# A three-way split output product, a full-height warm-up and a new order of jobs in a fused attention and quaternion kernel

## The reference, cut to what matters

```python
qkv = x @ Wqkv.T + bqkv
attn = softmax(q @ k.T / 4)
coh = sigmoid(tanh(concat(x, cond) @ Wc1.T + bc1) @ Wc2.T + bc2)
mod = attn * coh / (sum(attn * coh) + 1e-8)
fa = softmax(layernorm(relu(cond @ We1.T) @ We2.T) @ pe.T)
mod = (1 - 0.21) * mod + 0.21 * fa
x1 = x + (mod @ v) @ Wout.T + bout
out = x1 + rotate(gate(x1))
```

## Time and profile before

| what | us |
|---|---|
| median of 3 runs | 286.6 |
| lowest and highest | 285.88, 288.35 |
| the profiled execution, device time | 284.87 |
| its span, first to last instruction | 282.2 |
| mean granted clock of TensorE | 0.994 |

### The profile page before, as it was taken

One profiled execution on the slowest core, in us unless ns is written; L12 is line 12 of the kernel. 1 busy time (PEld: TensorE's weight loads), 2 busy tenths in 40 slices (PEclk: granted clock), 3 DMA queues, 4 the chain that ended last, 5 costly groups with the idle time before them and its releaser, 6 DMA issues.

```text
span 282.2 us, 4292 instructions
## 1 busy us (share of the span) xinstructions
PE 258.2 (92%) x1579; PEld 127.6 (45%) x1579; DVE 197.8 (70%) x232; ACT 168.7 (60%) x214; POOL 158.0 (56%) x143
## 2 busy tenths in 40 slices
PE   8999898989989878998989989989998999899984
PEld 7446543433544333635444444445453444344333
DVE  5689878557758567577677858876788677758323
ACT  3341654757566854475755884567656677586850
POOL 3950499999999499998000099980024079910000
PEclk9999999999979999999999999999999999999999
DMA  7854543300191005631270003400302500101002
GB/s 208 277 175 146 181 135 114 114 2 3 53 251 35 1 0 146 178 90 38 77 244 21 1 9 111 144 2 2 112 1 99 165 0 31 48 1 38 2 0 74
DMA packets 16787, 23.49 MB, mean 83 GB/s; under 512 B 2488, under 2 KB 8504, under 8 KB 16768
## 3 DMA queue, kind: packets, MB, share of 16 engines
q1 hardware_dynamic: 15936, 22.55, 26.1%
q10 hardware_dynamic: 832, 0.69, 0.8%
HBM read 8.41 MB, written 2.11 MB: 37 GB/s over the span
## 4 chain that ended last, share of the span: by engine, by line
PE 68%; ACT 11%; DVE 10%; issue 6%; DMA 2%; POOL 1%; ACTq 1%; SPq 0%; DVEq 0%; POOLq 0%
PE o_ps L1109 16%; PE job_ps L862 15%; PE pair_ps L1082 11%; ACT probs L541 9%; PE pair_ps L1094 8%; DVE maxima L686 5%; PE job_ps L996 4%; PE pair_ps L862 2%; DMA w_raw<-wqkvT 2%; PE job_ps L932 2%; DVE qk_lo L702 2%; PE pair_ps L970 1%; PE job_ps L962 1%; ACTq L585 1%; ACT max_rows L581 1%
## 5 line engine op out<-in xcount | busy, mean ns | idle before, releaser
L686 DVE TENSOR_REDUCE maxima<-pair_ps 128x2 f32<-128x1024 f32 x128 | 153.0, 1220 | 52.4 <-PE pair_ps L1082 51.9
L541 ACT ACTIVATE probs<-pair_ps 128x1024 f32<-128x1024 f32 x128 | 125.8, 1024 | 44.1 <-PE pair_ps L1094 37.0
L1109 PE MATMUL o_ps<-probs,vals 128*32 128x512 f32 x512 | 68.2, 604 | 0.2
L1094 PE MATMUL pair_ps<-stack 49*128 49x512 f32 x256 | 53.9, 441 | 6.0 <-ACT probs L541 3.9
L1082 PE MATMUL pair_ps<-stack 48*128 48x512 f32 x256 | 54.5, 446 | 2.6 <-ACT probs L541 1.5
L1094 PEld LDWEIGHTS pair_ps<-stack 49*128 49x128 f32 x256 | 24.0, 185 | 27.4 <-ACT probs L541 10.4
L1082 PEld LDWEIGHTS pair_ps<-stack 48*128 48x128 f32 x256 | 24.0, 186 | 24.0 <-issue 12.5
L400 POOL TENSOR_TENSOR x_lo<-x_raw,x_hi 128x1024 fp32r<-128x1024 f32 x3 | 7.1, 2373 | 46.2 <-ACT x_hi L547 46.2
L417 POOL TENSOR_TENSOR vals<-v_new,row 128x256 f32<-128x256 f32 x16 | 11.4, 732 | 32.8 <-ACT v_new L573 20.1
L516 POOL TENSOR_TENSOR prod<-amap,x_tok 128x1024 f32<-128x1024 f32 x12 | 28.5, 2377 | 0.9
L1109 PEld LDWEIGHTS o_ps<-probs,vals 128*32 128x32 f32 x512 | 10.1, 108 | 20.9 <-issue 19.6
(11 more groups left out here) (159 smaller groups left out, 305.3 us busy)
## 6 DMA issues: line engine op xcount, KB each, us to landing
stack<-qk_hi SPq DMA_DIRECT2D x64, 128.0 KB, 2.9
stack<-qk_lo SPq DMA_DIRECT2D x32, 128.0 KB, 2.9
x_tok<-x SPq DMA_DIRECT2D x4, 512.0 KB, 4.3
out<-y SPq DMA_DIRECT2D x8, 256.0 KB, 2.4
x_raw<-xT SPq DMA_DIRECT2D x3, 512.0 KB, 5.4
fa_now<-fa_rows SPq DMA_DIRECT2D x4, 256.0 KB, 3.5
row<-rows SPq DMA_DIRECT2D x1, 544.0 KB, 5.6
x_raw<-xT ACTq DMA_DIRECT2D x1, 512.0 KB, 4.9
```

Source lines behind the costliest of these rows:

```text
L541: nc.scalar.activation(probs[:, t % 4, :, :], ps[:, :, :], ACT.Exp, scale=SCALE).then_inc(exp_done, 1)
L686: nc.vector.tensor_reduce(maxima[:, gg % 2, :, pair, i], pair_ps[SLOT["S", u]][:, :, :], AX_X, ALU.max, negate=True).then_inc(s_reduced, 1)
L1094: ins = nc.tensor.matmul(pair_ps[SLOT["T", t]][:, a, :], stack[64 * a:64 * a + ROWS + 1, 1, p, j * P:(j + 1) * P], stack[64 * a:64 * a + R ...
L1109: ins = nc.tensor.matmul(o_ps[h * VW:(h + 1) * VW, :], vals[:, j, gg % G * HG + h, :], probs[:, (2 * k + h // 2) % 4, h % 2, :], start=(j ...
```

## The change

- The output product of batches 0 to 2 is a `split_product`: GpSimd splits `oT` (two halves of features for each batch) and `wf` into high and low parts, and TensorE runs three single passes. The parts of `oT` lie in the two columns of `stack` that the direct products used. The splits stand in GpSimd's order after the step of the next batch that OUT_SPLIT_STEPS names. The last batch keeps the fp32 product.
- `y` lies in `w_raw` instead of in a tensor of its own.
- The warm-up's ones have 128 rows, and TensorE starts when they are written.
- The q and k weights are split by ScalarE (high) and VectorE (low) instead of by GpSimd; a memset of `stack` moves from VectorE to GpSimd.
- All lists of runs, jobs and weighings are replaced; LATE is empty; X_HIGH_PAUSE is 3 instead of 6, HEAD 12 instead of 13, FORE_PAUSE 40 instead of 43.

In the new lists (first pauses again 0, 26, 48, 70), `out0` and `out1` stand in pauses 46 and 56 for batch 0 (39 and 44 before), 74 and 77 for batch 1 (61 and 68), and 96 and 99 for batch 2 (83 and 90).

```diff
@@ -36,34 +36,37 @@
-FIRST_RUNS = ("- S SS SS SS SS S SS TSTST SS TS S TSSSS T TS S ST TT TT TS ST TTS ST S STT TS").split()
-RUNS = ("TSS STT TSS SST STS TST TST TST SST TSTTS SS TST ST TSS STT TST STS STS STT ST STT ST").split()
-LAST_RUNS = ("STS TST STS STT STS TSS TSTS TST TSS STT ST TST TTS STS ST TSSTS STT ST T TST TSS TSS").split()
-TAIL_RUNS = ("TT T T T T T T TT TT").split()
...
-JOB_PAUSES = {"q0": -15, "k0": -13, "v0": -10, "q1": -5, "k1": -2, "v1": 0, "coh0": 2, "coh1": 3, "max0": 5,
-              "z": 7, "max1": 10, "zt": 14, "tok0": 15, "max2": 16, "field": 16, "max3": 22, "tok1": 23,
-              "back0": 26, "tok2": 28, "tok3": 31, "back1": 34, "out0": 35, "out1": 42}
-FIRST_PAUSES = {"dq0": 0, "dk0": 0, "q0": 0, "k0": 1, "dq1": 2, "dk1": 2, "cond": 2, "v0": 3, "q1": 4, "k1": 5,
-                "max0": 6, "coh0": 6, "v1": 7, "norms": 7, "fpre": 8, "coh1": 9, "max1": 12, "fpair": 12,
-                "z": 17, "max2": 18, "zt": 19, "tok0": 19, "flog": 20, "tok1": 23, "max3": 27, "field": 30,
-                "tok2": 32, "back0": 32, "tok3": 34, "back1": 37, "out0": 39, "out1": 44}
-LAST_PAUSES = {"q0": -14, "k0": -12, "v0": -5, "q1": -4, "v1": 2, "k1": 3, "max0": 5, "coh0": 7, "coh1": 8,
-               "max1": 11, "max2": 15, "field": 15, "z": 16, "zt": 18, "tok0": 19, "max3": 22, "tok1": 24,
-               "back0": 27, "tok2": 31, "tok3": 42, "back1": 48, "out0": 85, "out1": 86}
...
-WEIGH_AFTER = [1, 2, 1, 1, 0, 1, 1, 0, 1, 1, 2, 2, 0, 1, 0, 0]
-LAST_WEIGH_AFTER = [1, 0, 0, 2, 1, 1, 2, 1, 2, 0, 2, 3, 1, 0, 0, 3]
-HEAD = 13
+FIRST_RUNS = ("- SS SS SS SS SSS STSS STTST STSTS SST TSS ST ST TTS ST ST T T S S T S T T S T").split()
+RUNS = ("STS STS STS STS TST STS TSTSTS STT TTS TST TST TSTSS TTS TST TST STS SSS ST TT S TS T").split()
+LAST_RUNS = ("STS TSS STS TST STS STS TSTS STS TST TST TST STS TS TST TST STS ST TTS STS T S T TS S T T").split()
+TAIL_RUNS = ("TT TT TT T T T T T T").split()
...
+JOB_PAUSES = {"q0": -16, "k0": -14, "q1": -11, "coh0": -7, "v0": -6, "k1": 0, "coh1": 1, "v1": 2, "z": 4,
+              "max0": 5, "max1": 9, "zt": 14, "max2": 16, "tok0": 17, "field": 19, "max3": 21, "tok1": 25,
+              "tok2": 28, "back0": 32, "tok3": 34, "back1": 35, "out0": 48, "out1": 51}
+FIRST_PAUSES = {"dq0": 0, "dk0": 0, "q0": 0, "k0": 0, "dq1": 1, "dk1": 1, "q1": 2, "k1": 2, "v0": 3, "v1": 3,
+                "cond": 3, "coh0": 4, "max0": 5, "fpre": 5, "coh1": 6, "norms": 7, "fpair": 8, "z": 9,
+                "max1": 10, "zt": 11, "field": 12, "tok0": 13, "flog": 14, "max2": 18, "tok1": 24, "max3": 27,
+                "back0": 29, "tok2": 33, "tok3": 38, "back1": 39, "out0": 46, "out1": 56}
+LAST_PAUSES = {"q0": -15, "k0": -11, "v0": -7, "v1": -6, "q1": 0, "coh0": 1, "k1": 2, "max0": 5, "max1": 11,
+               "coh1": 15, "max2": 16, "z": 17, "zt": 18, "tok0": 21, "max3": 25, "tok1": 27, "tok2": 31,
+               "field": 34, "back0": 35, "tok3": 39, "back1": 41, "out0": 42, "out1": 43}
...
+WEIGH_AFTER = [0, 1, 1, 1, 1, 0, 3, 2, 3, 2, 2, 0, 0, 0, 1, 1]
+LAST_WEIGH_AFTER = [0, 0, 1, 0, 2, 0, 0, 3, 3, 0, 1, 2, 3, 1, 3, 4]
+HEAD = 12
 TAIL = 6
-FORE_PAUSE = 43
...
-X_HIGH_PAUSE = 6
...
-LATE = ("k0", "k1", "out0", "out1", "q0", "q1")
...
+OUT_SPLIT_STEPS = [(10, 10), (3, 6), (12, 12)]
...
+FORE_PAUSE = 40
...
+X_HIGH_PAUSE = 3
...
+LATE = ()
@@ -211,14 +214,17 @@
         dir_part = o_tok[:, :, :].rearrange("p i e -> p (i e)").rearrange("p (n s) -> p n s", n=2).bitcast(F32R)
-        y = sb("y", [P, 2, IT, E])
+        y = w_raw[:, :, :].rearrange("p n (i e) -> p n i e", i=IT)
+        oT_hi, oT_lo = (stack[:, side, DIRECT:DIRECT + KT, :] for side in range(2))
+        wf_hi = sb("wf_hi", [P, KT, E], F32R)
+        wf_lo = sb("wf_lo", [P, KT, E], F32R)
...
         n_half = sb("n_half", [CD, 2])
-        n_ones = sb("n_ones", [CD, P])
+        n_ones = sb("n_ones", [P, P])
@@ -247,7 +253,8 @@
             sem, ("ld_x", "ld_w64", "ld_row", "ld_small", "ld_we2", "ld_wc2", "ld_pe", "ld_wo", "ld_tok"))
-        ones_done, w_split = sem("ones_done"), sem("w_split")
+        ones_done, ones_more, w_split = sem("ones_done"), sem("ones_more"), sem("w_split")
+        wqk_hi_done, wqk_lo_done = sem("wqk_hi_done"), sem("wqk_lo_done")
@@ -260,6 +267,7 @@
         norm_step, fvec_done, oT_ready = sem("norm_step"), sem("fvec_done"), sem("oT_ready")
+        oT_hi_done, oT_lo_done, wf_parts = sem("oT_hi_done"), sem("oT_lo_done"), sem("wf_parts")
@@ -338,7 +346,7 @@
                 if half < HALF_SLOTS:
-                    sp.wait_ge(ones_done, 1 if half < 2 else 2)
+                    sp.wait_ge(*((ones_done, 1) if half < 2 else (ones_more, 1)))
@@ -417,15 +425,32 @@
                                         bias.unsqueeze(1).to_broadcast([P, IT, HG, HD]), ALU.add).then_inc(v_ready, 1)
+            def split_out(b, blk):
+                n = KT * b + blk + 1
+                pool.wait_ge(oT_ready, n)
+                nc.gpsimd.tensor_copy(oT_hi[:, blk, :], oT[:, blk, :]).then_inc(oT_hi_done, 1)
+                pool.wait_ge(oT_hi_done, n)
+                nc.gpsimd.tensor_tensor(oT_lo[:, blk, :], oT[:, blk, :], oT_hi[:, blk, :].bitcast(F32),
+                                        ALU.subtract).then_inc(oT_lo_done, 1)
...
+            steps = [0] * B
...
+            def step_done(b):
+                steps[b] += 1
+                if b:
+                    for blk, n in enumerate(OUT_SPLIT_STEPS[b - 1]):
+                        if n == steps[b]:
+                            split_out(b - 1, blk)
...
+            chain(nc.gpsimd.memset(n_ones[:, :], 1.0))
             chain(nc.gpsimd.memset(n_half[:, :], -0.5))
-            chain(nc.gpsimd.memset(n_ones[:, :], 1.0))
...
             pool.wait_ge(v_blank, 2)
-            split_weights(0, 0, 2 * E, ld_qk)
-            split_weights(1, 2 * E, 3 * E, ld_wv)
-            split_weights(2, 3 * E, 4 * E, ld_wc)
+            nc.gpsimd.memset(stack[:, 1, 8:DIRECT, :].bitcast(F32), 1.0).then_inc(ones_more, 1)
+            split_weights(0, 2 * E, 3 * E, ld_wv)
+            split_weights(1, 3 * E, 4 * E, ld_wc)
@@ -465,7 +490,8 @@
             chain(nc.gpsimd.tensor_scalar(q_all[:, 1, :, :, :], q_all[:, 0, :, :, :], -1.0, None, ALU.mult))
-            pool.wait_ge(w_split, 6)
+            pool.wait_ge(w_split, 4)
+            pool.wait_ge(wqk_lo_done, 1)
@@ -504,30 +530,42 @@
             pool.wait_ge(wf_done, 1)
+            nc.gpsimd.tensor_copy(wf_hi[:, :, :], wf[:, :, :]).then_inc(wf_parts, 1)
+            pool.wait_ge(wf_parts, 1)
+            nc.gpsimd.tensor_tensor(wf_lo[:, :, :], wf[:, :, :], wf_hi[:, :, :].bitcast(F32),
+                                    ALU.subtract).then_inc(wf_parts, 1)
...
                                               ALU.add))
+                step_done(b)
...
                     chain(nc.gpsimd.tensor_tensor(dst, a, s, ALU.mult))
+                    step_done(b)
...
                         chain(nc.gpsimd.tensor_tensor(y_b, y_b, tmp, ALU.add))
+                        step_done(b)
...
                 nc.gpsimd.tensor_tensor(y_b, y_b, tmp, ALU.add).then_inc(y_done, 1)
+                step_done(b)
...
                     x_low(b + 1)
+                    step_done(b)
...
                     values(b, g)
+                    step_done(b)
                 sum_values(b)
+                step_done(b)
                 values(b, 3)
+                step_done(b)
@@ -663,6 +701,8 @@
             x_high(0)
+            act.wait_ge(ld_qk, 16)
+            nc.scalar.activation(w_hi[:, :, 0:2 * E], w_raw[:, :, 0:2 * E], ACT.Copy).then_inc(wqk_hi_done, 1)
@@ -830,7 +870,9 @@
                                     ALU.subtract).then_inc(x_lo_done, 1)
-            nc.vector.memset(stack[:, 1, 8:DIRECT, :].bitcast(F32), 1.0).then_inc(ones_done, 1)
+            dve.wait_ge(wqk_hi_done, 1)
+            nc.vector.tensor_tensor(w_lo[:, :, 0:2 * E], w_raw[:, :, 0:2 * E], w_hi[:, :, 0:2 * E].bitcast(F32),
+                                    ALU.subtract).then_inc(wqk_lo_done, 1)
@@ -880,7 +922,10 @@
                 pe.wait_ge(x_lo_done, b + 1)
-                pe.wait_ge(w_split, {"q": 2, "k": 2, "v": 4, "coh": 6}[kind])
+                if kind in ("q", "k"):
+                    pe.wait_ge(wqk_lo_done, 1)
+                else:
+                    pe.wait_ge(w_split, {"v": 2, "coh": 4}[kind])
@@ -983,19 +1028,19 @@
                 half, b = int(job[0][3]), job[1]
-                pe.wait_ge(wf_done, 1)
-                pe.wait_ge(oT_ready, KT * (b + 1) + (half if b == B - 1 else 0))
                 if b == B - 1:
+                    pe.wait_ge(oT_ready, KT * (b + 1) + half)
...
                     return
+                pe.wait_ge(wf_parts, 2)
+                pe.wait_ge(oT_lo_done, KT * (b + 1))
                 claim(job)
-                ps, done = bank(job), job_filled
...
                     i = 2 * half + tile
-                    for k in range(KT):
```

(11 more changed lines are left out.)

## The result

| executions | kernel before | changed kernel |
|---|---|---|
| median, us | 286.24 | 277.05 |
| lowest and highest, us | 285.77, 288.35 | 274.91, 281.57 |

The ratio is 0.964, with a 95% interval of 0.9559 to 0.9721; by the medians it is 9.2 us faster. Ratios here leave out executions more than 1.5% above the fastest of the same kernel, medians keep them. The forecast was 281.7.

What follows compares the result with a forecast made beforehand. TensorE, busy 92% of the span, was taken as the bound, with ScalarE and VectorE costing by arriving late. Terms summed to -4.9 us from 284.87, to 280.0, plus 1.73 for the median: 281.7 us, range 278.3 to 288.5.

Steps and rivals of the forecast that it cites:

- Part 1: Output product on TensorE: six jobs go from 1.93 to 1.63 us as single passes, -1.8 us.
- Part 2: Splits on GpSimd: hidden beside TensorE, batch 1's values about 6 us earlier; 0 charged, up to +2.
- Part 3: Start: full-height warm-up and moved weights' split bring the first projection from 11.47 to 9.85; -1.6 us, or -0.4.
- Part 4: Low granted clock near 80 us: gone or a second one, -1.6 to +1.6; half taken, -0.8 us.
- Part 5: Tail, last 15.2 us before the last weighing: output jobs fill TensorE's time spent on ScalarE; -1.0 us.
- Part 6: LATE emptied: VectorE low parts no longer stand behind the next reduction; -1.0 us, bounds -2.8 to +1.
- Part 7: Placement's added waits: longer runs of score passes +2.0 us, batch 0's second maxima job +0.8.
- C: Rival: slower, as dense runs in the three-buffer ring set the pace, up to 1.9 us each; 289.5 us, chance 0.12.
- Part 8: Second stretch's excess over the third: small TensorE waits of 5.8 us, a quarter of them gained, -1.5 us.
- Rival D: Better: the second stretch loses only what the third loses, shrinking by 7.4 us; 277.0 us, chance 0.16.
- B: Rival: only arithmetic is left, parts 1 and 3 at -1.8 and -0.4, 4 to 8 cancel; 284.4 us, chance 0.22.

Runs made afterwards that it cites:

- fp32_out: Changed kernel with the fp32 output product in all batches and no splits on GpSimd; median 278.06 us, 275.2 at full clock.
- old_lists: Changed kernel with the old lists of runs, jobs and weighings, and split steps set to suit them; median 287.36 us, 284.8 at full clock.
- after_third: The changed kernel run a third time, nothing altered; median 277.63 us, its profiled execution 273.93 us.
- new_lists_only: Kernel before with only the new lists, HEAD, FORE_PAUSE, X_HIGH_PAUSE and empty LATE; median 282.6 us, 277.5 at full clock.
- new_lists_late_old: Kernel before with the new lists, but LATE holding q0, q1, k0 and k1; median 291.55 us, 287.1 at full clock.
- start_old_lists: Changed kernel with the old lists, the fp32 output product and no splits; median 283.12 us, 282.4 at full clock.
- first_old: Changed kernel with the old lists for batch 0 up to its pause 25, new ones behind; median 291.02 us, 280.8 at full clock.

## Why the prediction was wrong, point by point

The forecast was a change of -4.9 us, -0.8 of it by the clock. At full clock the change is 284.1 to 273.6, -10.5, and the clock takes some of it back. By steps:

- **Part 1, output product: right.** -1.8 was forecast, -1.6 measured. The job starts at 132.29 and the next pass at 133.92:

```profile
132.29 0.74 PE L904 MATMUL job_ps<-wf_hi,stack 128*128 128x256 f32 x4
...
133.92 0.49 PE L1139 MATMUL pair_ps<-stack 49*128 49x512 f32 x2
```

  1.63, as the value product gave; all six take 1.60 to 1.63 here and 1.89 to 1.93 in fp32_out. The Trainium skill (FP8 and Floating Point Precision, TensorE Precision Notes) gives true fp32 four passes; the prediction's estimate of 1.45 from it wasn't reached.
- **Part 2, splits: right on the new lists.** No output job waits for GpSimd there. Its values of batch 1 start at 102.92, 5.1 us before those of the earlier trace rows (6 forecast):

```profile
102.92 2.12 POOL L425 TENSOR_TENSOR vals<-v_new,row 128x256 f32<-128x256 f32 x3
```

  The cover is the lists' doing: with output jobs where they stood it was gone, at a price of about 4 us (old_lists).
- **Part 3, start: right, mechanism and size.** First projection at 9.92 (9.85 forecast), where before had 11.47. Undone alone, the height is worth 1.6 at full clock and the engines of the split 1.4; they are one gain, since either wait ends at the same projection. All local edits but the output product take 277.5 to 275.2, 2.3; whether the 0.7 beyond 1.6 is an effect or the error of the estimate no run says.
- **Part 4, clock: wrong in sign.** Near 80 the clock is 1.00, as the step wanted. But two of three profiles have a low stretch of 17 us between 27 and 53, and ten of fourteen executions a mean clock below 0.990. The median execution of before lies 2.1 us above its value at full clock (286.24 against 284.1), that of the change 3.4 (277.05 against 273.6). So the term is about +1.3, not -0.8, near the end of its bounds.
- **Part 5, tail: right where it looked.** In the last 15.2 us before the last weighing TensorE's idle time falls from 0.71 to nothing, with 14.0 us of work by the costs before and all 15.2 filled after:

```profile
246.58:261.78 15.20, 15.20 (x112) 7.36 (x110) 3.94 (x10) 12.08 (x14) 0.00 (x0) 1.00 0.11 36
```

  That is 0.7 to 1.2 for the -1.0. Over the whole of batch 3 the idle time falls by 1.7; the step didn't look at the rest.
- **Part 6, LATE emptied: the step that failed.** It took three weight-load waits for the price of LATE, and a reduction 0.74 later for the price of its absence, both read off the old lists, and came to -1.0. The measured terms at full clock are +4.8 on the old lists and -9.6 on the new (277.5 less 287.1; -8.3 at the least). It has no worth by itself: it goes with the distance that a list leaves between a projection and the next job in the one bank `job_ps`. The wait that the step should have priced is the one that the new order would bring with LATE filled, 9.5 us in 12 waits, and that the old order had mostly avoided. Without this step the new lists are no gain at all: with LATE filled they stand 1.7 to 3.0 us above the kernel before.
- **Part 7, what the placement adds: right for the runs, wrong for the maxima job and in what it does to the sum.** A run of six does take what C gave it. Its passes begin at 92.27 and the weighing behind it at 95.64:

```profile
92.27 0.49 PE L1139 MATMUL pair_ps<-stack 49*128 49x512 f32 x2
...
94.30 0.50 PE L1127 MATMUL pair_ps<-stack 48*128 48x512 f32 x2 [0.69 <-ACT probs L579]
...
95.21 0.50 PE L1127 MATMUL pair_ps<-stack 48*128 48x512 f32 x2 [0.17 <-ACT probs L579]
95.64 1.06 PE L1154 MATMUL o_ps<-probs,vals 128*32 128x512 f32 x8
```

  3.37 for 1.6 of matmuls and switch, 1.8 over (up to 1.9 by C). The second maxima job of batch 0, priced at +0.8, costs nothing: from 47.97 to its pass at 50.55 are 2.6 us, and no wait stands before the pass. It is the first maxima job, for which the step had no term, that makes TensorE wait:

```profile
30.47 0.28 PE L962 MATMUL job_ps<-ident,maxima 128*16 128x128 f32 x1
...
34.51 0.50 PE L1139 MATMUL pair_ps<-stack 49*128 49x512 f32 x2 [1.85 <-DMA stack<-max_rows]
...
47.97 0.28 PE L962 MATMUL job_ps<-ident,maxima 128*16 128x128 f32 x1
...
50.55 0.40 PE L1139 MATMUL pair_ps<-stack 49*128 49x512 f32 x2
```

  Yet the new order with all of that has 6.6 us less. Waits were counted where new ones would come and not where old ones would go.
- **Part 8, batch 1's excess: right in sign, too small, and measured against a wrong floor.** The step's stretch, from the first score pass of batch 1 to that of batch 2, and the one behind it, before and in after_third:

```profile
74.32:141.22 66.90, 60.70 (x383) 30.18 (x382) 46.11 (x54) 41.05 (x50) 53.47 (x30) 0.97 0.34 92
141.22:201.80 60.58, 57.29 (x375) 27.91 (x373) 45.47 (x53) 40.05 (x49) 26.82 (x16) 1.00 0.23 75
...
76.19:135.55 59.36, 56.62 (x379) 27.47 (x376) 45.52 (x51) 40.58 (x51) 54.08 (x33) 1.00 0.35 87
135.55:192.51 56.96, 55.00 (x378) 27.10 (x378) 45.48 (x52) 39.44 (x49) 23.30 (x17) 1.00 0.23 66
```

  TensorE's idle time in the first falls from 6.2 to 2.7, 3.5 against 1.5 forecast, and in the second from 3.3 to 2.0. The floor was miscounted. The third stretch of the earlier trace rows was priced with 6 projections and 16 weighings, but its trace holds 5 and 15: by the same costs it lost some 4.9 us, not 2.3. Nor do the second and third stretch hold the same work; the second has a projection and more than a weighing over, some 2.9 of the 7.4 us between them.

Parts 5 to 8 together were -0.7 and are -6.6 (new_lists_only at full clock). Parted by new_lists_late_old, that is 5, 7 and 8 at +1.7 to +3.0 for a forecast of +0.3, and part 6 at -8.3 to -9.6 for -1.0. That is nearly the whole miss, and the clock's term, 2.1 off the other way, hid a part of it. Rival D had the time nearly to the point, and its stretch does shrink by 7.5 us (66.90 to 59.36) for 7.4 forecast. That is in part luck: 1.6 of it is the low clock, 3.5 idle time, and the rest work that now stands in other stretches, while the later stretches, which D left alone, gain too. C's mechanism stands in the rows and decides nothing. B's 2.2 us for parts 1 and 3 fit no run: the local parts give 3.9 on the new lists and nothing on the old, where the start without the splits gives 1.7 (start_old_lists). Its premise, that 4 to 8 cancel, falls with new_lists_only.

What stays open: which of the moves in the lists carry the 6.6 us. The idle times say that each batch gains once its weighings run, the two-by-two of lists and LATE says that VectorE's place for the low parts is needed for it, and first_old was too broken a mixture to say more. HEAD, X_HIGH_PAUSE and FORE_PAUSE were never changed apart from the lists, and `y` in `w_raw` never by itself.
